# Fourteen expert tiles moved ahead of the phase boundary, and a tile table made across partitions, in an attention and mixture-of-experts kernel

## What is computed

```python
def reference(x, adj, Wq, Wk, Wv, Wo, gate_W, gate_b, expert_W, expert_b):
    h = layernorm(x)
    a = einsum('bhnd,bhmd->bhnm', heads(h @ Wq.T), heads(h @ Wk.T)) * 512**-0.5 + 2 * adj
    x = x + merge(softmax(a) @ heads(h @ Wv.T)) @ Wo.T
    h = layernorm(x)
    p = softmax(maximum(h @ gate_W + gate_b, 1e-4))
    two = top_k(p, 2)
    w = maximum(p, 0.1); w = w / sum of w over the two; comb = where(two, w, 0)
    y = einsum('bsd,edf->bsef', h, expert_W) + expert_b
    return x + einsum('bsef,bse->bsf', y, comb) / 2
```

## Time and profile before

| | us |
|---|---|
| median of 3 runs | 1673.18 |
| lowest and highest | 1671.38, 1673.78 |
| the profiled execution | 1670.63 |
| its span, first to last instruction | 1668.8 |
| barrier between the phases released | 1202.0 |
| first product of phase two | 1209.04 |
| last product of phase two, about | 1654 |

### The profile page before, as it was taken

How to read it: one execution, slowest core, us unless ns; L and a number is a source line. 1 busy time by engine, 2 the same in 40 slices (tenths; PEclk the granted TensorE clock), 3 DMA queues, 4 the chain that set the end, 5 groups by cost and what they waited for, 6 DMA issues and landing times. The chain is left out here.

```text
span 1668.8 us, 43148 instructions
## 1 busy us (share of the span) xinstructions
PE 1571.8 (94%) x11856; PEld 1388.9 (83%) x11856; DVE 1195.6 (72%) x4698; ACT 987.6 (59%) x3093; POOL 970.8 (58%) x1693
## 2 busy tenths in 40 slices
PE   6999999999999999999999999976189999999996
PEld 6899999899999999999999999965168888888885
DVE  5677878878888788878888788787535555555554
ACT  4778787788877788777887878776111111111111
POOL 3245665666656666566665666557335656565554
PEclk9999999999999999999999999987599999999998
DMA  6987787887878888788887878793658898898886
GB/s 227 233 222 215 232 247 231 252 249 226 253 227 256 246 225 250 225 241 231 225 245 228 243 224 224 223 288 128 221 101 168 169 171 159 166 170 165 162 160 101
DMA packets 188619, 351.84 MB, mean 211 GB/s; under 512 B 20960, under 2 KB 30304, under 8 KB 188256
## 3 DMA queue, kind: packets, MB, share of 16 engines
q1 hardware_dynamic: 135520, 238.47, 51.0%
q0 software_dynamic: 29680, 69.55, 21.6%
q10 hardware_dynamic: 23184, 41.05, 7.9%
HBM read 189.48 MB, written 159.52 MB: 209 GB/s over the span
## 5 line engine op out<-in xcount | busy, mean ns | idle before, releaser
L654 ACT ACTIVATE prob<-prob,nmax 128x128 f32<-128x128 f32 x1024 | 398.6, 393 | 164.6 <-DVE amax L803 135.5
L1060 POOL TENSOR_TENSOR prob<-prob,rinv 128x512 f32<-128x512 f32 x256 | 261.7, 1043 | 223.8 <-DVE rinv L820 223.5
L799 DVE CUSTOM_DVE_ANT_0 prob<-ps_s,bias 128x128 f32<-128x128 f32 x1024 | 237.7, 287 | 165.3 <-PE ps_s L516 127.9
L1256 POOL DMA_INDIRECT out<-yt,token x135 | 211.1, 1564 | 196.1 <-DMA out<-yt,token 67.5
L1194 ACT ACTIVATE xgT_hi<-ps_x 128x512 fp32r<-128x512 f32 x135 | 80.7, 598 | 385.5 <-PE ps_x L1167 335.0
L1178 PE MATMUL ps_y<-we,xgT_hi 128*128 x540 | 226.2, 419 | 6.3 <-DVE xgT_lo L1213 6.3
L1179 PE MATMUL ps_y<-we,xgT_hi 128*128 x540 | 214.1, 396 | 0.0
L1180 PE MATMUL ps_y<-we,xgT_lo 128*128 x540 | 214.0, 396 | 0.0
L654 ACT ACTIVATION_READ_ACCUMULATOR prob<-prob,nmax 128x1 f32 x1024 | 194.4, 190 | 0.0
L803 DVE TENSOR_REDUCE amax<-prob 128x4 f32<-128x512 f32 x256 | 175.7, 686 | 8.9
L1069 POOL DMA_INDIRECT x_lists<-xn,pos x128 | 135.5, 1059 | 68.8 <-DVE pos L924 40.5
(11 more groups left out here) (152 smaller groups left out, 4198.6 us busy)
## 6 DMA issues: line engine op xcount, KB each, us to landing
ks<-kq_parts SPq DMA_DIRECT2D x192, 256.0 KB, 4.2
qs<-kq_parts SPq DMA_DIRECT2D x192, 256.0 KB, 6.4
xg<-x_lists ACTq DMA_DIRECT2D x135, 260.5 KB
xin<-x SPq DMA_DIRECT2D x64, 256.0 KB, 7.0
kq_parts<-kT_hi SPq DMA_DIRECT2D x32, 512.0 KB, 4.0
kq_parts<-kT_lo SPq DMA_DIRECT2D x32, 512.0 KB, 5.0
kq_parts<-qT_hi SPq DMA_DIRECT2D x32, 512.0 KB
kq_parts<-qT_lo SPq DMA_DIRECT2D x32, 512.0 KB
```

The lines of the kernel that those rows point to most:

```text
L654: last = nc.scalar.activation(prob[:, r, c, h, :], prob[:, r, c, h, :], ACT.Exp, bias=nmax[:, r, i:i + 1], scale=-1.0, accum_out=rsum[:, r ...
L799: last = nc.vector.tensor_tensor_reduce(out=prob[:, r, c, h, :], in0=ps_s[c % 2][:, P * h:P * h + P], in1=bias[:, b % 4, :], scale=-1.0, s ...
L1060: tt(prob[:, r, q], prob[:, r, q], rinv[:, r, HC * q:HC * q + HC].unsqueeze(2).to_broadcast([P, HC, P]), ALU.mult)\
L1256: pool.indirect_dma_start(out=out, out_offset=bass.IndirectOffsetOnAxis(ap=token[:, m, :], axis=0), in_=yt[:, r, :], in_offset=None, compu ...
```

## The change

1. **Fourteen tiles ahead.** After 56 of the 64 batches are scattered, the fullest list has at least 56*2/8 = 14 full tiles. DVE finds that expert (`choose_early`, turn 60) and SP loads its weights as the first of the eight, to slot 0. The first fourteen tiles of its list are loaded by ACT, five in one go at (62, 0) and the others one by one; transposed by PE at the (t, c) of `T_AT` in the bank of the X2 transposes; multiplied at those of `Y_AT`, tiles 0 to 8 in the drain; written back with the weight applied by ACT; and added to `out` by POOL at those of `ADD_AT`. Tiles 9 to 13 follow at the start of phase two, before its other tiles. The bias is a 13th product, of a row of ones with the bias row, in fp32.
2. **The table of the other 121** is made with a tile in each partition, so that its operations on DVE have 8 elements instead of 1080; four transposes on PE and one copy bring it to one partition. What depends on the chosen expert is prepared at turn 62 (`prepare_table`).
3. Buffers are laid out anew, with places that outlive phase one. Phase two's own code is the same but for the count and the slot number in the table's new row.

```diff
+KNOWN = 56
+FULL = KNOWN * K // E
+LEFT = TILES - FULL
+AHEAD = 5
...
+        T_AT = {(64, 1): 0, (64, 3): 1, (65, 1): 2, (65, 3): 3, (66, 1): 4, (67, 2): 5, (67, 3): 6, (68, 1): 7, (68, 2): 8, (68, 3): 9}
+        Y_AT = {(64, 3): 0, (65, 1): 1, (65, 3): 2, (66, 1): 3, (67, 2): 4, (67, 3): 5, (68, 1): 6, (68, 2): 7, (68, 3): 8}
...
+        def early_load(act, j):
+            m = j % AHEAD
+            if j == 0:
+                act.wait_ge(rows_done, 1)
+                act.wait_ge(X_full, B)
+                for k in range(4):
+                    act.wait_ge(scattered[k], 32 * (KNOWN // 4))
+            if j >= AHEAD:
+                act.wait_ge(added_e[m], 16 * (j // AHEAD))
+            row = act.value_load(early_i[0:1, j:j + 1], min_val=0, max_val=ROWS - P)
+            act.dma_start(xg_e[:, m, :], x_lists[bass.ds(row, P), :]).then_inc(xg_e_in[m], 16)
...
+        def early_products(pe, j, bank):
+            pe.wait_ge(xgT_e_lo_done, j + 1)
...
+            for c in range(DC):
+                hi, lo = (v["we"][:, bass.ds(at * (2 * DC * D) + (DC * i + c) * D, D)] for i in range(2))
+                nc.tensor.matmul(bank, xgT_e_hi[:, r, c, :], hi, start=c == 0, stop=False)
+                nc.tensor.matmul(bank, xgT_e_hi[:, r, c, :], lo, start=False, stop=False)
+                nc.tensor.matmul(bank, xgT_e_lo[:, r, c, :], hi, start=False, stop=False)
+            nc.tensor.matmul(bank, one_row, b_row[:, :], start=False, stop=True).then_inc(y_e_full, 1)
+
+        def early_out(act, j, bank):
+            m = j % AHEAD
+            act.wait_ge(y_e_full, j + 1)
+            act.wait_ge(comb_e_step, 2 * j + 2)
+            nc.scalar.activation(xg_e[:, m, 0:D], bank, ACT.Identity, bias=zero_col[:, :], scale=comb_e[:, m:m + 1]).then_inc(y_e_done, 1)
...
+                    if (t, c) == (KNOWN + 4, 3):
+                        choose_early()
+                    if (t, c) == (KNOWN + 6, 3):
+                        prepare_table()
...
+            pe.wait_ge(cols_done, 1)
+            pe.wait_ge(pT_done, DC * B)
+            for i in range(4):
+                last = nc.tensor.transpose(ps_t[0:1, P * i:P * i + P], choice[:, 10, i:i + 1], ident)
+            last.then_inc(cols_full, 1)
...
+    def pe_in_b(pe):
+        for j in IN_B:
+            if j + 1 < FULL:
+                pe.wait_ge(xgT_e_lo_done, j + 1)
+                early_transposes(pe, j + 1)
+            pe.wait_ge(y_e_done, j - 1)
+            early_products(pe, j, bank_in_b(j))
...
         @block.tensor
         def _(pe):
+            early["pe"](pe)
+            pe.wait_ge(early["y_e_done"], FULL)
```

More of the change, by code:

```diff
@@ L283, in phase_a @@
+        count_c, equal, selected, below, order_f, slot, d_slot, skip_more, taken = (choice[:, i, :] for i in range(9))
+        top_count, top_key, chosen, first_row, row_base = (choice[:, 9, i:i + 1] for i in range(5))
         RSTD, ROUTE, PLACE = 8, 24, 4
@@ L457, in transposes @@
                 kind, n, part = unit
+                if kind == "T":
+                    wait_bank(before_in(small, 1, t, c))
+                    early_transposes(pe, n)
+                    return
                 if kind == "X":
@@ L635, in read_transposes @@
                 kind, n, part = unit
+                if kind == "T":
+                    early_hi(act, n)
+                    return
                 if kind == "X":
@@ L722, in _ @@
                         rows_for_nobody((t - 7) // 4)
+                    for j in LOAD_AT.get((t, c), ()):
+                        early_load(act, j)
                     if (t, c) in HI_AT:
@@ L975, in _ @@
             dve.wait_ge(pT_full, DC * B)
-            free = prob[0:1].rearrange("p a c h m -> p (a c h m)")
-            one, n_e, past, skip = (free[:, E * i:E * i + E] for i in range(4))
-            passed, more = (free[:, at_:at_ + a * b].rearrange("p (a b) -> p a b", a=a) for at_, a, b in ((4 * E, TILES, E), (4 * E + TILES * E, E, B)))
-            tab_f = free[:, 4 * E + (TILES + B) * E:4 * E + (TILES + B) * E + 3 * TILES].rearrange("p (r t) -> p r t", r=3)
+            more = prob[:, 1, 0].rearrange("p h m -> p (h m)").rearrange("p (e b) -> p e b", e=E)
+            one, n_e, past, skip, passed, part, sums = (prob[:, 1, 1, 0, E * i:E * i + E] for i in range(7))
+            cols = choice[:, 10, :]
+            row = const[:, C_ROW:C_ROW + 1]
             step = [0]
@@ new lines, in _ @@
+            link(tt(more, n_e.unsqueeze(2).to_broadcast([P, E, B]), const[:, C_MULT:C_MULT + B].unsqueeze(1).to_broadcast([P, E, B]), ALU.is_gt))
+            link(total(n_e, more))
+            link(tt(n_e, n_e, taken, ALU.subtract))
+            link(nc.vector.tensor_tensor_scan(past, one, n_e, 0.0, ALU.mult, ALU.add))
+            link(nc.vector.scalar_tensor_tensor(out=skip, in0=n_e, scalar=-float(P), in1=skip_more, op0=ALU.mult, op1=ALU.add))
+            link(tt(passed, past, over(row), ALU.is_le))
@@ new lines, in _ @@
+            link(total(cols[:, 0:1], passed))
+            link(tt(part, passed, skip, ALU.mult))
+            link(total(cols[:, 1:2], part))
+            link(tt(part, passed, d_slot, ALU.mult))
+            link(total(cols[:, 3:4], part))
+            link(tt(part, past, over(row), ALU.is_lt))
+            link(total(sums[:, 0:1], part))
+            link(tt(cols[:, 1:2], cols[:, 1:2], row_base, ALU.add))
+            link(tt(cols[:, 3:4], cols[:, 3:4], slot[:, 0:1], ALU.add))
+            link(tt(cols[:, 2:3], cols[:, 0:1], sums[:, 0:1], ALU.not_equal))
@@ L1121, in phase_b @@
     x_lists, out = v["x_lists"], v["out"]
+    early = v["early"]
     R = RING
@@ L1195, in body @@
                     t = tile(g, j + N)
+                    if g == -1 and j < 5:
+                        early["act"](act, j)
                     if t.valid:
```

250 lines of the change are left out of this document (206 added, 44 removed).

## The result

The changed kernel takes 1680.37 us (median of 7 runs, 1678.19 to 1684.71), the kernel before on the same chip 1673.18 (7 runs, 1670.77 to 1675.40). The ratio is 1.0051 with a 95% interval of 1.0041 to 1.0061: slower by 0.5%, or 7 to 9 us, where 1671 was forecast. The profiled execution has a span of 1676.4 us, 7.6 more than that of before, and took 1678.19.

The account below looks back on a forecast made before the run. TensorE was taken to bound phase two, with waits for the last pairs' chain in the drain. Sum -45.2 + 23.1 + 20.0 = -2.1 against the median 1673.2: 1671 us, range 1657 to 1684.

Parts of the forecast that it names:

- Tiles taken out of phase two: Phase two on TensorE: fourteen tiles fewer at 3.23 us each, -45.2 us, called sure.
- Start of phase two: From barrier release to first of the 121 tiles: tiles 9 to 13 come first, 27.0 instead of 7.0, +20.0 us.
- The release: Barrier between the phases: released at 1225.1 instead of 1202.0, +23.1 us.
- Turns 60 to 63: End of phase one: expert choice and five ACT loads move place(29) from 1149.5 to 1153.5.
- The drain: From place(29) to tile 8's end on TensorE: 12.4 + 37.0 + 5 + 6 = 60.4 us, ending at 1213.9.
- The boundary: Tile 8's end to release: ACT's zero writes behind its write-back, last at 1219.1, then 6.0 us to 1225.1.
- the old waits each get a tile ahead of them and vanish: TensorE in the drain: old waits of 2.13, 4.10, 3.46 and 4.09 vanish behind tiles; 6 us of waits left.
- (a): Drain and barrier: TensorE stays warm and full, zero rows land in 3.4 instead of 6.0; 1662, chance 0.30.
- (b): POOL's in-order queue becomes the chain, adds delaying the last norms and loads: +9.4 us, 1680, chance 0.24.
- (c): Drain: waits only move behind their tiles, 16.4 us stay instead of 6, loads cost all 5.3; 1684, chance 0.08.
- The prediction's indirect issue of 2.85: POOL's queue: an indirect issue takes 0.96 us, but 2.85 when something holds it up.

Follow-up runs that it names:

- e3_route: Changed kernel with the last pair's routing (choice, weights, places) put ahead of tiles; ratio to the kernel before 1.0034.
- e8_sp: Changed kernel with loads of tiles 5 to 10 on SP, the last pair's routing ahead of tiles, and ACT's zero writes earlier; ratio to the kernel before 1.0015.
- e16_pool_delay: Changed kernel with three more POOL operations, their result unused, ahead of the root computation of batch 62; ratio to the kernel before 1.0091.
- e5_no_tiles: Changed kernel without the fourteen early tiles; choice, order of the weights and table stay; ratio to the kernel before 0.9738.
- e12_all: e8_sp with adds of tiles 0 and 1 behind the roots, tile 7's behind the barrier, and a cheap, late-awaited bias product; ratio to the kernel before 0.9980.

## Why the prediction was wrong, step by step

The forecast was 1671 with -2.1 against before; the profiled span gives +7.6. Its direction was wrong, and its range, 1657 to 1684, held the time. By its own terms:

- **Tiles taken out of phase two**, -45.2. Measured 415.5 us from the first product to the end instead of 459.8: -44.3. Right.
- **Start of phase two**, +20.0. Measured 27.6 instead of 6.8 from release to first product: +20.8. Right as a sum. Its parts are off against each other: a tile took 4.39 instead of 4.07, 1.6 more for five (0.15 of each 0.32 is the bias row; the 0.37 and 2.80 also left 0.06 of the 3.23 out), and cold start, waits and the way to the first of the 121 tiles took 5.6 instead of 6.7.
- **The release**, +23.1. Measured 1233.3 instead of 1202.2: +31.1. This is the step that failed, by 8.0 of the 9.7 us. It was built of the drain and the boundary:
  - *Turns 60 to 63*: place(29) was forecast at 1153.5 and came at 1151.85. That is no sign of less work, since this execution was ahead already: its place(28) is at 1105.15, that of before at 1108.56. Between the two places it took 5.8 us more than before, where 4.0 were forecast.
  - *The drain*: 60.4 us from place(29) to the end of tile 8 were forecast, 68.6 came. TensorE was busy for 58.2 instead of 54.4. Nine tiles at 4.39 instead of 4.07 are 2.9 of that, and the low clock took, by what is left, 5.9 instead of 5: tile 4 alone, whose products had a pace of 0.43 instead of 0.23 behind the wait of 5.30, has about 2 of it. TensorE was idle for 10.5 instead of 6.0. I had left 2.9 for `gT` and seen ACT's load and weight copy ahead of it, but not that this load has an add's landing to wait for: 5.30.
  - *The boundary*: 11.2 forecast, 12.9 measured. The size is nearly right, and the mechanism is half of it. I had ACT's zero writes behind tile 8, and they were there: their issue ended at 1227.1 and SP arrived at 1232.6. But POOL ended 0.5 us later: its scatters stood behind places that VectorE took up 7.5 us late, and the add of tile 7 behind the scatters. That path stood in no term. e3_route shows that either of the two holds the barrier: with the places early POOL is ready at 1225.7, and the zero rows hold it to 1230.4.

The common fault of the step "the old waits each get a tile ahead of them and vanish" is that I read it for TensorE alone. The other engines got pieces of tiles ahead of the last pair's steps too, and those pieces wait for TensorE. Mending that order, and no tile less, gave 6.0 us (e8_sp), of a loss of 8.5 against the kernel before.

Of the rivals, **(a)** is right in the clock only: 0.95 and 0.84 instead of 0.64, with a fall just where TensorE waited 5.30. The trace agrees with what the prediction quotes of the Trainium skill (TensorE: Matmul & The Clock Gate, "HAM oscillation — how this bites in real kernels"): a granted clock of 0.95 while no wait was longer than 1.20 us, and 0.52 from 1190 to 1200 us, around the wait of 5.30. But the rest at the barrier stayed, and the kernel is slower all the same. **(b)** gave the right time, 1680, and its mechanism is half of the truth. POOL had the mean of batch 62 before 1170.6 and began at 1174.76; e16_pool_delay shows that the queue has next to no slack. But in the changed kernel only 1.20 and 0.41 us of it reached TensorE at the norms, not 2.8 each, and moving the adds away brought nothing. That it gave the right time is luck. **(c)** is nearest in what one sees, waits of 10.5 us in the drain, though for another reason: half of them is the one wait for `gT`, which stood on ACT behind the load of a tile that waited for an add.

What stays open is how the 6.0 us of e8_sp divide into its three parts. Singly they are 2.8, 2.3 and nothing, each within about 3 us. Open too is how much of the last 12.8 us is the transfers' own time, with the DMA engines full for ten of them.

## What to carry to other kernels

Work that is put into the gaps of a drain costs little only if, on every engine, the steps of the chain that releases the barrier stand ahead of the pieces of filler; look for each such step on each queue, not at the engine with the gap alone. Only as many pieces of filler belong ahead of a barrier as it has rest: behind it they cover nothing, and here each of them cost 1.2 us more than in its old place. When several engines arrive at one barrier close together, an experiment that moves one is worth only the distance to the next: in e3_route POOL came 7.4 us earlier and the release 2.7. Look at the arrivals in each profile, not only at the time.

## What the hardware showed that I had not expected

- **An add issued just ahead of the barrier is paid there.** POOL's DRAIN takes 1.71 us in the kernel before and in e5_no_tiles, which have no adds there, and 2.7 to 7.3 in the runs that have. It ends 8.9 us after the last add was issued (1224.23 to 1233.1), in e3_route 6.8 (1218.89 to 1225.7), in e12_all 11.2, although the add's own record is 1.6 us long. No row shows the landing itself; that the DRAIN waits for it is the reading of these numbers. The Trainium skill (Perfetto Trace Analysis, "DMA Instruction — SWDGE (GPSIMD)") says that such a record ends when the descriptors are made and not when the data has moved; the trace agrees, with the numbers above.
- **An add that a load waits for is slow in the drain.** The add of tile 1, issued at 1179.62, released the load of tile 6 at 1190.9: 11 us, where the adds of phase two are 5.7 apart.
- **A small POOL operation beside a large one of VectorE lasts as long as that one.** In the changed kernel the cast at 1171.05 and the root's step at 1180.76 take 1.74 and 1.64 us where the shortest of their lines take 0.18, and both end within 0.05 us of a 128x2048 operation of VectorE (1170.43 to 1172.75 and 1180.07 to 1182.36). The step L1251 of e16_pool_delay is a third. The prediction's indirect issue of 2.85 stood beside such an operation too (1162.23 to 1165.10 in the kernel before). So part of POOL's lateness for the norms comes from the splitting of the weights; no run moved those operations.
- **A product of two partitions is not free.** With 512 columns in fp32r it has a pace of 0.42 us behind it, where the full ones have 0.23; the fp32 row has 1.05.
